# A three-layer CIN tower with its opening put in another order: weights prepared behind block 0's gathers, loads and sums reordered

## What is computed

```python
def cin(inputs, W0, b0, W1, b1, W2, b2):
    B, F, D = inputs.shape          # 512, 40, 32
    h, outs = inputs, []
    for i, (W, bias) in enumerate(params):
        x = jnp.einsum('bhd,bmd->bhmd', h, inputs).reshape(B, -1, D)
        y = jax.nn.relu(jnp.einsum('oi,bid->bod', W, x) + bias[None, :, None])
        if i != 2:
            h, direct = jnp.split(y, 2, axis=1)   # 100 maps on, 100 out
        else:
            direct = y
        outs.append(direct)
    return jnp.concatenate(outs, axis=1).sum(-1)
e = jnp.stack([tbl_f[ids[:, f]] for f in range(40)], axis=1)
h = jnp.concatenate([cin(e, ...), dense_ctx], axis=1)
h = jnp.maximum(h @ W_top1 + b_top1, 0.0)
h = jnp.maximum(h @ W_top2 + b_top2, 0.0)
y = h @ W_top3
```

## Time and profile before

| | us |
|---|---|
| median of 3 runs | 2821.92 (2819.53 to 2822.87) |
| the profiled execution | 2822.93 |
| its span | 2821.1 |
| PE busy | 2775.4 (98% of the span) |
| DVE busy | 2637.9 (94%) |
| ACT busy | 1500.6 (53%) |
| POOL busy | 858.7 (30%) |

### The profile page before, as it was taken

One profiled execution on the slowest core, in us unless ns is written; L12 is line 12 of the kernel. 1 busy time (PEld: TensorE's weight loads), 2 busy tenths in 40 slices (PEclk: granted clock), 3 DMA queues, 4 the chain that ended last, 5 costly groups with the idle time before them and its releaser, 6 DMA issues.

```text
span 2821.1 us, 54038 instructions
## 1 busy us (share of the span) xinstructions
PE 2775.4 (98%) x19012; PEld 2758.2 (98%) x19012; DVE 2637.9 (94%) x1945; ACT 1500.6 (53%) x1880; POOL 858.7 (30%) x700
## 2 busy tenths in 40 slices
PE   5999999999999999999999999999999999999999
PEld 4999999999999999999999999999999999999997
DVE  6999999999999999999999999999999999999995
ACT  4555555555555555555555555555555555555553
POOL 5433332332332332332323323323323323333100
PEclk9999999999999999999999999999999999999999
DMA  7333333433433433333334334334333334334330
GB/s 210 85 83 84 86 94 78 94 87 76 99 88 75 100 84 82 97 84 85 93 79 94 87 78 97 89 75 102 85 78 99 85 82 95 85 86 94 85 78 18
DMA packets 286025, 249.66 MB, mean 89 GB/s; under 512 B 31286, under 2 KB 284446, under 8 KB 285893
## 3 DMA queue, kind: packets, MB, share of 16 engines
q1 hardware_dynamic: 216310, 200.56, 25.4%
q0 software_dynamic: 65712, 45.56, 12.1%
q10 hardware_dynamic: 3972, 3.17, 0.4%
HBM read 140.74 MB, written 4.20 MB: 51 GB/s over the span
## 4 chain that ended last, share of the span: by engine, by line
PE 94%; POOL 2%; DVE 1%; DMA 1%; issue 1%; SPq 0%; ACT 0%; another core or an unknown queue 0%; DVEq 0%; ACTq 0%; POOLq 0%
PE acc L809 62%; PE acc L811 29%; POOL gathered L445 1%; PE z_ps L826 1%; PE hid_ps L822 1%; DVE tails L721 1%; DMA acc_copy<-acc_copy 1%; DVE product L716 1%; PE acc L880 0%; SPq L380 0%; DMA gathered<-in_table,rows_all 0%; PE hid_ps L903 0%; DMA hid_rep<-hid 0%; ACT acc_copy L528 0%
## 5 line engine op out<-in xcount | busy, mean ns | idle before, releaser
L809 PE MATMUL acc<-weights,heads 126*128 126x400 f32 (+1 forms) x9088 | 2694.1, 364 | 16.3 <-DVE tails L721 16.2
L811 PE MATMUL acc<-weights,tails 126*128 126x200 f32 (+1 forms) x9088 | 2321.6, 255 | 0.0
L522 ACT ACTIVATE heads<-product 126x1024 fp32r<-126x1024 f32 (+2 forms) x1152 | 1198.1, 1047 | 1021.5 <-PE acc L811 507.3
L811 PEld LDWEIGHTS acc<-weights,tails 126*128 126x128 f32 (+1 forms) x9088 | 1740.8, 192 | 0.0
L809 PEld LDWEIGHTS acc<-weights,heads 126*128 126x128 f32 (+1 forms) x9088 | 1712.9, 188 | 19.7 <-issue 10.0
L721 DVE TENSOR_TENSOR tails<-product,heads 126x1024 fp32r<-126x1024 f32 (+2 forms) x1152 | 1348.9, 1204 | 1.4 <-ACT heads L522 1.1
L716 DVE TENSOR_TENSOR product<-hid_rep,x_rep 126x2048 f32<-126x2048 f32 x510 | 1167.4, 2289 | 96.5 <-PE acc L811 64.8
L453 POOL DMA_DIRECT2D acc_copy<-acc_copy x189 | 235.0, 1244 | 1719.8 <-ACT acc_copy L528 1716.4
L445 POOL DMA_INDIRECT gathered<-in_table,rows_all x320 | 510.8, 1596 | 101.4 <-issue 97.1
L536 ACT ACTIVATE y_relu<-acc_copy 128x400 f32<-128x400 f32 x192 | 102.4, 533 | 217.0 <-DMA acc_copy<-acc_copy 215.0
L528 ACT ACTIVATE acc_copy<-acc 128x800 f32<-128x800 f32 x192 | 158.7, 827 | 9.8 <-PE acc L811 7.7
(11 more groups left out here) (26 smaller groups left out, 118.2 us busy)
## 6 DMA issues: line engine op xcount, KB each, us to landing
x_rep<-x_rows SPq DMA_DIRECT2D x512, 120.0 KB
hid_rep<-hid SPq DMA_DIRECT2D x511, 120.0 KB
x_pairs<-x_rows SPq DMA_DIRECT2D x191, 280.0 KB
acc_copy<-acc_copy POOLq DMA_DIRECT2D x189, 200.0 KB
hid_rep<-hid SPq DMA_DIRECT2D x511, 5.0 KB
x_pairs<-x_rows SPq DMA_DIRECT2D x63, 120.0 KB
gathered<-in_table,rows_all POOLq DMA_INDIRECT x320
raw_weights<-in_w SPq DMA_DIRECT2D x8, 500.0 KB, 6.1
```

Of the source, the lines that this page charges most:

```text
L522: act.activation(heads[0:rows, ring % HEADS_RING, 0:tiles, :], product[0:rows, ring % PRODUCT_RING, 0:tiles, :], ACT.Copy).then_inc(heads_ ...
L809: nc.tensor.matmul(acc[:, at.parity, c, 0:2 * LAYER], dims(heads[0:rows, ring % HEADS_RING, k, :], c), w, start=(q == 0 and k == 0), stop= ...
L811: last = nc.tensor.matmul(acc[:, at.parity, c, LAYER:2 * LAYER], dims(tails[0:rows, ring % PRODUCT_RING, k, :], c), w[:, 0:LAYER], start=F ...
```

## The change

- **Held preparation.** DVE starts the sums and tails of the weights only when POOL has issued block 0's five gathers (`first_rows_asked`). On ACT the first two chunks of w1 come ahead of layer 0's two chunks; `split_place` gives each chunk its place in the new order for the waits.
- **42 rows.** `x_pairs` is loaded as 42 x 3 = 126 rows instead of 120, the row of ones moves to row 126, and the weight rows 120 to 125 are zero. The DMAs' outer size is 42 instead of 40.
- **w2's splits.** All seven chunks of w2 are now made later: three inside layer 1 and four inside layer 2 of iteration 2. SP loads two of them where it loaded seven, and the other five behind the load of block 1's `hid`.
- **x_rep.** The second half for block 0 is issued behind the load of block 0's `hid`.
- **POOL.** Its share of block 0's first `hid_rep` load goes ahead of block 3's store. For blocks 4 and 5 all three adds go ahead of the gathers; from block 6 on the order is as before.
- **Block 1's first copy.** In iteration 1 ACT's `copy_acc` of layer 0 comes ahead of the heads of groups 2 and 3, and its relu ahead of the heads of group 6.

```diff
+FIELDS_PADDED = 42
+ROWS0 = SHIFTS * FIELDS_PADDED
-OPERAND_ROWS = (PAIRS0 + 1, PAIRS + 1, PAIRS + 1)
+OPERAND_ROWS = (ROWS0 + 1, PAIRS + 1, PAIRS + 1)
...
             if i == "start":
-                return list(range(split_until[0])) + w1[:4]
+                return w1[:2] + list(range(split_until[0])) + w1[2:4]
             if (i, layer) == (0, 0):
                 return w1[4:]
-            if (i, layer) == (2, 0):
-                return w2[:3]
-            if (i, layer) == (2, 1):
-                return w2[3 + q // 2:4 + q // 2]
+            if (i, layer) == (2, 1) and q > 0:
+                return w2[q // 2 - 1:q // 2]
+            if (i, layer) == (2, 2) and q < GROUPS - 2:
+                return w2[(3, 4, 5)[q // 2]:(4, 5, 7)[q // 2]]
             return []
+
+        split_order = split_after("start") + split_after(0, 0)
+        split_order += list(range(len(split_order), len(prep)))
+        split_place = [split_order.index(n) for n in range(len(prep))]
...
-            parts = [(x_pairs[0:PAIRS0, 0, :],
-                      block_rows(duo, parity, 0, FIELDS).unsqueeze(1).to_broadcast([FIELDS, SHIFTS, COLS]))]
+            parts = [(x_pairs[0:ROWS0, 0, :],
+                      block_rows(duo, parity, 0, FIELDS_PADDED).unsqueeze(1).to_broadcast([FIELDS_PADDED, SHIFTS, COLS]))]
             for j in range(SHIFTS):
-                rows = block_rows(duo, parity, j, FIELDS)
-                parts.append((x_pairs[j:PAIRS0:SHIFTS, 1:1 + TILES0, :],
+                rows = block_rows(duo, parity, j, FIELDS_PADDED)
+                parts.append((x_pairs[j:ROWS0:SHIFTS, 1:1 + TILES0, :],
                               bass.AP(tensor=rows.tensor, offset=rows.offset,
-                                      ap=[[COLS, FIELDS], [SHIFTS * COLS, TILES0], [1, COLS]])))
+                                      ap=[[COLS, FIELDS_PADDED], [SHIFTS * COLS, TILES0], [1, COLS]])))
...
                 if not whole and i == 0:
                     load_x_rep(0, 0, 0)
-                    load_x_rep(0, 0, 1)
...
                     for half in range(FLD_HALVES):
                         load_x_rep(duo, parity, half)
-                    load_weights(split_until[1], split_until[2])
+                    load_weights(split_until[1], split_until[1] + 2)
...
                     load_hid(0, (0, 2, 3) if not whole and i == 0 else range(HID_OUT))
+                    if not whole and i == 0:
+                        load_x_rep(0, 0, 1)
+                    if not whole and i == 1:
+                        load_weights(split_until[1] + 2, split_until[2])
...
             for b in range(FIRST):
                 for k in range(FLD_DMA):
                     gather(b, k, rows_all[:, b, k:k + 1], first_gathered[b])
+                if b == 0:
+                    pool.memset(marker[:, blocks - 1:blocks], 0.0).then_inc(first_rows_asked, 1)
             for b in range(2, FIRST):
                 pool.wait_ge(first_gathered[b], GATHERS)
                 for part in stored_parts(b, b):
                     pool.dma_start(*part).then_inc(first_stored[b], 16)
+                if b == 2:
+                    pool.wait_ge(hid_copied[0], 1)
+                    for part in hid_parts(0, 1):
+                        pool.dma_start(*part).then_inc(hid_first_loaded, 16)
             add(0)
-            pool.wait_ge(hid_copied[0], 1)
-            for part in hid_parts(0, 1):
-                pool.dma_start(*part).then_inc(hid_first_loaded, 16)
...
             for b in range(FIRST, blocks):
                 first = 1 + (b - FIRST) * 3
-                ahead = 1 if b == FIRST + 1 else 0
-                for k in range(ahead):
-                    gather(0, k, rows_all[:, b, k:k + 1], x_gathered)
-                add(first)
-                for k in range(ahead, FLD_DMA):
+                sums_ahead = 3 if b < FIRST + 2 else 1
+                for n in range(sums_ahead):
+                    add(first + n)
+                for k in range(FLD_DMA):
                     gather(0, k, rows_all[:, b, k:k + 1], x_gathered)
                 pool.wait_ge(x_gathered, (b - (FIRST - 1)) * GATHERS)
-                add(first + 1)
-                add(first + 2)
+                for n in range(sums_ahead, 3):
+                    add(first + n)
...
                 for q in range(2) if first else ():
                     make_heads(*first, q)
+                if odd is None and i == 1:
+                    copy_acc(*l0)
                 if before:
                     copy_acc(*before)
...
-                if l0 and first:
+                if l0 and first and not (odd is None and i == 1):
                     copy_acc(*l0)
...
                 split_heads(*split_now(6))
+                if odd is None and i == 1:
+                    relu(*l0)
                 if first:
                     make_heads(*first, 6)
-                if l0 and first:
+                if l0 and first and not (odd is None and i == 1):
                     relu(*l0)
...
                 for q in range(2) if second else ():
                     make_heads(*second, q)
+                split_heads(*(split_after(i, 2, 0) if odd is None else ()))
...
                     for q in range(2, 4):
                         make_heads(*second, q)
+                    split_heads(*(split_after(i, 2, 2) if odd is None else ()))
                     copy_acc(*first)
                     make_heads(*second, 4)
                     make_heads(*second, 5)
+                    split_heads(*(split_after(i, 2, 4) if odd is None else ()))
                     relu(*first)
...
-                    dve.wait_ge(weight_heads, n + 1)
+                    dve.wait_ge(weight_heads, split_place[n] + 1)
...
+            dve.wait_ge(first_rows_asked, 1)
             for n in range(2):
...
-                    pe.wait_ge(weight_tails, split_until[0] + q - 1 if layer == 0 else
-                               split_until[layer - 1] + (GROUP * q + GROUP - 1) // PREP_TILES + 1)
+                    chunk = q if layer == 0 else split_until[layer - 1] + (GROUP * q + GROUP - 1) // PREP_TILES
+                    pe.wait_ge(weight_tails, max(split_place[:chunk + 1]) + 1)
```

More of the change, by code:

```diff
@@ L174, in cin_kernel @@
         rows_ready = sem("rows_ready")
+        first_rows_asked = sem("first_rows_asked")
         x_gathered = sem("x_gathered")
@@ L338, in _ @@
                 sp.dma_start(dst, src).then_inc(consts_loaded, 16)
-            for row in (x_pairs[PAIRS0:PAIRS0 + 1, :, :].rearrange("p a c -> p (a c)"),
+            for row in (x_pairs[ROWS0:ROWS0 + 1, :, :].rearrange("p a c -> p (a c)"),
                         x_rep[PAIRS:PAIRS + 1, :, :, :].rearrange("p a b c -> p (a b c)")):
@@ L925, in lay_out @@
     w0a[:PAIRS0] = w[:, i, m].transpose(2, 1, 3, 0).reshape(PAIRS0, TILES0, LAYER)
-    w0a[PAIRS0, 0] = arr("L0_rec_b0")
+    w0a[ROWS0, 0] = arr("L0_rec_b0")
     w0b[:PAIRS0] = w[:, m, i].transpose(2, 1, 3, 0).reshape(PAIRS0, TILES0, LAYER)
```

## The result

| | before | after |
|---|---|---|
| median, same session (14 runs each) | 2820.97 (2816.99 to 2824.05) | 2828.94 (2818.93 to 2831.41) |
| the profiled execution | 2822.93 | 2828.77 |
| its span | 2821.1 | 2826.9 |
| block 3's layer 0 starts on PE | 120.80 | 122.28 |
| block 4's layer 0 starts on PE | 166.05 | 174.42 |

The changed kernel is slower, by a little but clear of the noise: ratio 1.0024, 95% interval 1.0017 to 1.0032. (It is not the quotient of the two medians, 1.0028: the executions after fall in two groups.) The prediction had 2819.0, faster. Of the 14 executions after, twelve took 2826.68 us or more and two took 2818.93 and 2820.46; the profiled one is of the twelve.

The account below looks back on a forecast made before the run. PE bounds the kernel from 140 us on, so only earlier idle and low-clock time can be won: -1.1 at block 3's layer 0 and -1.9 make -3.0, 2819.9 profiled, median 2819.0 (own range 2815.5 to 2822.5; wider 2812.5 to 2829).

Parts of the forecast that it names:

- The landmark: Start of block 3's layer 0 on PE, 120.80 before; behind it PE is the bound except 1.94 us; forecast 119.7.
- 1.94: PE's idle time between 132 and 140 us; forecast to go because block 5's adds precede its gathers, -1.9.
- Block 0's opening: DVE held until block 0's five gathers are issued, so their data lands sooner: 0.8 us taken, bounds 0 and 2.6.
- Pair loads on 42 rows: Block 0's pair loads stream faster with 42 rows than 40: 0.9 us taken, product at 23.3 with the opening.
- Rival C: The opening moves nothing: weight loads hide the gathers, issue limits the pairs; 1.7 less won, 2820.7; chance 0.12 together with D, 2821 if the 1.94 stays.
- Block 0's first hidden product: DVE's first hidden product at 41.0 instead of 45.32, -4.3; PE's third group then starts without idle 1.76 or low clock.
- Block 1's copy ahead of two heads: Earlier copy on ACT removes DVE's 2.52 wait at the fold; layer-1 tails at 69.7, PE at 71.0, -9.4.
- What is given back: Later w2 tails (+4.4) and waits for ACT (+1.9) put block 1's layer 1 fold at 107.1, only 3.0 sooner.
- The one spell at the low clock: PE idles some 3 us in two pieces before block 3's layer 0; one more low-clock spell taken, +1.7.
- late fold: Block 1's layer 1 fold 0 to 2 us late because block 4's gathers delay the fourth add; 1 taken.
- rival B: Block 4's gathers get no pause and hold the fourth add; block 3's layer 0 at 132.0, total 2831; chance 0.20.
- POOL's order: Two of block 4's gathers held until 89, done at 96 to 98.5; block 5's adds before gathers remove the 1.94.

Follow-up runs that it names:

- e1: The changed kernel with POOL's order for block 5 as before the change; median 2820.74 us, ratio 1.0001 to the kernel before.
- e8: e1 with SP's store of block 1 issued behind the wait for block 0's pair loads; median 2820.68 us, ratio 0.9996 to the kernel before.
- e13: e12 with the fifth add on POOL moved ahead of the fifth of block 5's gathers; median 2814.86 us, ratio 0.9987 to the kernel before.
- e4: The changed kernel with the seventh add between block 5's first and second gather, block 6's gathers without an add ahead; 2826.48 us, ratio 1.0017.
- e6: e1 with x_pairs loaded as 40 x 3 rows again; median 2823.39 us, ratio 1.0005 to the kernel before.
- e10: e8 with ACT's copy and relu of block 1's layer 0 back where they were; median 2818.18 us, ratio 1.0001 to the kernel before.
- e5: e1 with w2's loads and splits where they were before the change; median 2826.81 us, ratio 1.0017 to the kernel before.
- e9: e8 with ACT's w2 heads ahead of the heads of their pair in iteration 2's layer 2; 2822.34 us, ratio 1.0017 to the kernel before.
- e2: The kernel before with only the changed POOL loop, three adds ahead of the gathers for blocks 4 and 5; 2831.04 us, ratio 1.0020.
- e12: e9 with the fourth add on POOL ahead of all five of block 5's gathers; median 2817.68 us, ratio 0.9997 to the kernel before.

## Why the prediction was wrong

**The landmark held, but not alone.** The span less b4 is 2655.0 before, 2652.5 after, 2651.4 to 2653.2 in e1 and e8 to e13: what happens before b4 decides, as the prediction argued. (It is more, 2659.9, in e4, whose late add comes behind b4, and in the slow execution of e6.) The 2 to 3 us between them are PE's idle time in the loop, 2.21 before and 0.06 after; "in matmuls the extra rows cost nothing" was right, but their gain in the loop, about 2 us, was left out. The profiled execution took 2828.77 for a forecast 2819.9, 8.9 more: b3 came 2.6 later than forecast, from b3 to b4 it took 8.8 more (52.1 for 45.25 less 1.94), and the rest 2.5 less.

**Block 0's opening: -0.8 forecast, 0 measured,** because something other than the gathers' issue sets when they land. **Pair loads on 42 rows: -0.9:** the size is plausible (6.5 to 7.7 with the store behind, against 7.35, 7.5 and 8.8), though within the scatter, but the change lets block 1's store in among the loads, and 8.1 came out. This queue effect of the hold was not costed. The product started at 26.05, not 23.3. The Trainium skill's "DMA: Bandwidth & Descriptors", "Why a DMA increments its semaphore by 16 and not by 1", gave 1.1 by its rule of divisors. The direction agrees (middle values 6.9 with 42 rows, 7.5 with 40); no run here counts the engines, and the traces scatter too much to test the size. Rival C, that the opening moves nothing, was nearer than the forecast; the product came 1.05 later than before.

**Block 0's first hidden product** came at 43.30, 2.0 before's 45.32, not at 41.0; the 2.3 of difference come from the opening. That PE's third group follows without idle time or low clock was right.

**Block 1's copy ahead of two heads.** The tails of layer 1 came at 71.73 and PE at 73.09, 7.3 sooner than before, for 9.4 forecast; again 2.0 of it come from the opening. But the cause in the heading was wrong: e10 shows the copy's place worth no more than 0.65. With w2's work back where it was (e5) PE's layer 1 is at 80.64, so moving w2 is what it is; and there DVE's last wait, 4.56, comes behind the three tails of 3.4 us which the prediction counted, most likely for the load of `hid_rep` behind w2's loads. The prediction saw those loads only as a burden on the add.

**What is given back.** From those tails to the fold it took 39.0 us (71.73 to 110.74), against 31.1 + 4.4 + 1.9 = 37.4; DVE's pauses there sum to 2.9 instead of 1.9. The one spell at the low clock cost the 1.7 forecast. Block 3's layer 0 was at 122.28 for 119.7: 2.0 of this from the opening, 1.6 from here, less the 1.0 counted for a late fold that did not come. (The terms given for 119.7 add up to 119.6, and three quarters of rival B's 0.20 are 0.15, not 0.16; neither changes anything.)

**POOL's order: the step that failed.** For block 4 it counted a hold that did not happen: the five gathers passed from 81.61 to 90.01, close behind DVE's pauses of 0.41, 0.46 and 0.21 before 78.94, 80.80 and 87.97, for ACT's relu, for w2 and for `hid_rep`. For block 5 it wrote "the 1.94 goes" and counted -1.9 as pure gain. The 1.94 did go. But the same edit puts all five gathers of block 5 behind the sixth add and in front of the seventh, in a stretch where DVE runs unbroken from 122.6 to 141.0; the earlier trace rows had shown such holds, and the prediction did not ask what stands behind the gathers there. The prediction's own terms for rival B, counted from DVE's pause at 141.0 (0.9 + 4 x 1.25 + 1.5 + 3.8), would have put the add at 152.2, 4 us behind the 148 at which it was wanted. With the measured ones (131.50 + 10.46, four more gathers of 2.1 with 0.3 between, 3.1 for the landing, 3.8 for the store and marker) it is 158.5. PE lost 7.37 us, and at the lower clock some 2 more: b3 to b4 took 52.1 us, against 42.8 in e1. Rival B had the mechanism, with the wrong block: it named block 4. That its 2831 lies near 2828.94 is luck, since it had block 3's layer 0 at 132.0, where 122.28 came out.

**How long a hold lasts.** Holds of 8 to 14.66 us last over the ends of seven to twelve VectorE instructions. The Trainium skill's "SBUF — State Buffer", "SBUF: two separate sides", has the ports locked for one instruction; by that alone a gather would wait for one at most. The measurement decides against it.

## What to carry to other kernels

Ask of every queue what stands behind the instruction that can be held, not only what stands before it: a hold of 10.46 us in front of an awaited add cost 7.4 us of PE, and one of 14.65 us with the awaited add ahead of it cost nothing (e13). Where gathers pass by VectorE's pauses, removing VectorE's small waits can lose more than it gains (e9), so change queue order and pauses together (e13). And when a transfer is brought forward, look at what its neighbours in the queue now collide with.

## What the runs showed of the hardware

A gather by indirect DMA is let through soon after a pause of DVE and can be held in a long unbroken run. In e8's trace 129 gathers of over 1 us ended 0.75 to 1.08 us behind the start of a DVE instruction that followed the one before it without a pause (stops of 0.1 us and more count as pauses). For 127 of them one to five instructions had run since DVE's last pause, for one each six and eight. The held gather of the kernel after passed seven such boundaries, behind the seventh to thirteenth instruction, unreleased. What counts them is open.

Most holds ended 0.9 to 1.0 us behind the start of DVE's next pause, but three did not: e2's of 8.08, e12's and e13's. e12's ended at 115.08, and DVE's next pause is that before 118.81:

```profile
100.42 14.66 POOL L455 DMA_INDIRECT gathered<-in_table,rows_all  x1 [0.30 <-issue]
```

```profile
111.79 2.36 DVE L744 TENSOR_TENSOR tails<-product,heads 126x1024 fp32r<-126x1024 f32 x2
114.12 2.29 DVE L739 TENSOR_TENSOR product<-hid_rep,x_rep 126x2048 f32<-126x2048 f32 x1
...
118.81 2.29 DVE L739 TENSOR_TENSOR product<-hid_rep,x_rep 126x2048 f32<-126x2048 f32 x1 [0.40 <-PE acc L834]
```

It ended 0.97 us behind 114.12, where the new instruction overlaps the one before by 0.03 us. At every other boundary from 82 to 118 the overlap is 0.08 us or more. In e13 (114.40) and e2 (90.97) the hold ended in the same way, at the one boundary of its run with an overlap of 0.02 and 0.04. So a start later by some 0.05 us seems to do what a pause does; three cases suggest it, and no run tests it.

POOL's direct DMAs, its adds and stores, were not held: none of the 315 in any of the fifteen traces took over 1.41 us. In e5 DVE runs from 73.75 to 93.6 without a pause; the add goes through in the midst of it and the gather behind it does not:

```profile
84.87 1.17 POOL L461 DMA_DIRECT2D acc_copy<-acc_copy  x1 [4.58 <-ACT acc_copy L541]
86.34 8.25 POOL L453 DMA_INDIRECT gathered<-in_table,rows_all  x1 [0.30 <-issue]
```

Two kernels with such gathers ahead of adds (after, e2) had executions in two groups, whose medians lie 9.5 and 14.8 us apart; why, no trace shows.
